# Attention and feed-forward layer: the product with v moves ahead of each half step's scores for the exponentials

## What is computed

```python
q, k, v = jnp.split(jnp.einsum('bld,ed->ble', x, w_qkv), 3, axis=-1)
q = _rope(q.reshape(B, L, H, Dh))
k = _rope(k.reshape(B, L, H, Dh))
scores = jnp.einsum('blhd,bmhd->bhlm', q, k) * scale
attn = jax.nn.softmax(scores, axis=-1)
out = jnp.einsum('bhlm,bmhd->blhd', attn, v).reshape(B, L, D)
return jnp.einsum('bld,ed->ble', out, w_out)
```

## Time and profile before

| | |
|---|---|
| median of 3 runs | 2955.85 us (2955.6 to 2956.34) |
| the profiled execution | 2953.22 us, its span 2951.4 us |
| busy share of the span | PE 97%, DVE 91%, ACT 83%, POOL 18% |
| chain that ended last | PE 87%, ACT 5%, DVE 5% |
| reductions of the maxima (L1289) | 2048, mean 1213 ns |
| exponentials (L893) | 4096, mean 595 ns |

### The profile page before, as it was taken

How to read it: one execution, slowest core, us unless ns; L and a number is a source line. 1 busy time by engine, 2 the same in 40 slices (tenths; PEclk the granted TensorE clock), 3 DMA queues, 4 the chain that set the end, 5 groups by cost and what they waited for, 6 DMA issues and landing times.

```text
span 2951.4 us, 67323 instructions
## 1 busy us (share of the span) xinstructions
PE 2860.2 (97%) x27416; PEld 1057.3 (36%) x27416; DVE 2683.4 (91%) x2910; ACT 2463.5 (83%) x4609; POOL 522.7 (18%) x1087
## 2 busy tenths in 40 slices
PE   5999997999999999999999999999999999999999
PEld 4566663233333333333333333333333333333336
DVE  6676667999999999999999999999999999999952
ACT  4545542899999999999999999999999999999972
POOL 4666662000000000000000000000000000000000
PEclk8999997899999999999999999999999999999999
DMA  3233231111111111111111111111111111111125
GB/s 108 82 105 113 91 106 51 26 32 31 31 31 30 31 31 32 31 32 31 31 31 31 31 31 31 31 31 31 31 31 31 31 31 31 31 31 31 31 63 179
DMA packets 124601, 137.14 MB, mean 46 GB/s; under 512 B 43264, under 2 KB 103296, under 8 KB 124288
## 3 DMA queue, kind: packets, MB, share of 16 engines
q1 hardware_dynamic: 124288, 132.79, 16.5%
HBM read 88.15 MB, written 34.08 MB: 41 GB/s over the span
## 4 chain that ended last, share of the span: by engine, by line
PE 87%; ACT 5%; DVE 5%; issue 2%; DMA 1%; SPq 0%; POOL 0%; DVEq 0%; ACTq 0%; POOLq 0%
PE psum L714 37%; PE psum L679 20%; PE psum L739 17%; PE psum L589 5%; PE psum L561 4%; ACT probs L893 3%; PE psum L662 2%; DVE row_max L1289 2%; ACT acc_sb L872 1%; PE psum L604 1%; ACT hT L796 1%; DVE stats L1061 1%; DVE xnT L1085 1%; DVE h L1213 0%; ACT silu L809 0%
## 5 line engine op out<-in xcount | busy, mean ns | idle before, releaser
L1289 DVE TENSOR_REDUCE row_max<-psum 128x1 f32<-128x1024 f32 x2048 | 2332.2, 1213 | 24.0 <-PE psum L679 23.0
L893 ACT ACTIVATE probs<-psum 128x512 f32<-128x512 f32 x4096 | 2179.2, 595 | 162.3 <-PE psum L739 59.6
L714 PE MATMUL psum<-probs,v_op 128*32 128x256 f32 x15872 | 1296.6, 398 | 0.0
L739 PE MATMUL psum<-q_op,k_op 51*128 51x512 f16 x4096 | 854.0, 381 | 19.1 <-ACT probs L893 15.6
L679 PE MATMUL psum<-k_op,q_op 48*128 48x512 f16 x4096 | 807.6, 391 | 21.3 <-DVE row_max L1289 19.8
L679 PEld LDWEIGHTS psum<-k_op,q_op 48*128 48x128 f16 x4096 | 196.6, 93 | 874.9 <-DVE row_max L1289 570.1
L714 PEld LDWEIGHTS psum<-probs,v_op 128*32 128x32 f32 x15872 | 312.4, 108 | 523.4 <-issue 484.8
L739 PEld LDWEIGHTS psum<-q_op,k_op 51*128 51x128 f16 x4096 | 365.1, 94 | 256.8 <-ACT probs L893 66.9
L1046 POOL TENSOR_TENSOR acc_sb<-acc_sb,inv_rows 128x512 f32<-128x512 f32 x64 | 81.7, 1276 | 1686.9 <-DMA inv_rows<-inv_dram 1686.9
L589 PE MATMUL psum<-xnT,wf 128*128 128x512 f16 x768 | 178.8, 379 | 0.0
L803 ACT ACTIVATE parts<-qk_rot 128x512 f16<-128x512 f32 x64 | 40.1, 627 | 147.6 <-POOL qk_rot L969 147.6
(11 more groups left out here) (103 smaller groups left out, 1025.1 us busy)
## 6 DMA issues: line engine op xcount, KB each, us to landing
qk_dram<-staged SPq DMA_DIRECT2D x64, 256.0 KB, 4.8
q_op<-qk_dram SPq DMA_DIRECT2D x128, 128.0 KB
k_op<-qk_dram SPq DMA_DIRECT2D x128, 128.0 KB
x_ln<-in_x SPq DMA_DIRECT2D x16, 512.0 KB, 4.3
x_res<-in_x SPq DMA_DIRECT2D x16, 512.0 KB, 5.1
y_dram<-y_blk SPq DMA_DIRECT2D x16, 512.0 KB, 3.3
k_op<-qk_dram SPq DMA_DIRECT2D x128, 64.0 KB
q_op<-qk_dram SPq DMA_DIRECT2D x128, 64.0 KB
```

The lines of the kernel that those rows point to most:

```text
L714: mm = pe.matmul(bank(7)[32 * j:32 * j + 32, n0:n1], v_op[:, h % 2, t, :], probs[:, g3 % PROBS, j * BANK + n0:j * BANK + n1], start=(t == ...
L739: pe.matmul(bank(b), k_op[r:e, h % SLOTS, t * P:(t + 1) * P], q_op[r:e, h % SLOTS, j * BANK:(j + 1) * BANK], start=True, stop=True).then_i ...
L893: nc.scalar.activation(probs[:, g2 % PROBS, j * BANK:(j + 1) * BANK], bank(b), ACT.Exp, scale=to_score).then_inc(s2_used, 1)
L1289: nc.vector.tensor_reduce(row_max[:, hl % 2, t, half:half + 1], psum[:, 2 * half * BANK:(2 * half + 2) * BANK], AX.X, ALU.max).then_inc(s1 ...
```

## The change

In each half step of the TensorE program the half product with v is issued ahead of the two scores for the exponentials, where it stood behind them. In the first half step it stands directly behind the first scores for the maxima, in the second directly behind the second ones, ahead of the stabiliser's transpose where there is one. Nothing else is touched: the same instructions, the same waits on each, the same buffers. The lists of the other engines are the same word for word.

```diff
+            weigh_v(0)
             for j in range(4):
                 if j == 2:
-                    weigh_v(0)
                     if c < N1:
                         max_half(c, 1)
+                    weigh_v(1)
                     h = head_of(c, STAB_AT)
                     if h is not None:
                         pe.wait_ge(stab_step, STAB_STEPS * (h + 1))
...
                     item += 1
-            weigh_v(1)
             if c > N1:
                 project(c - N1 - 1)
```

## The result

The change is slower: 2986.73 us, median of 4 runs (2986.06 to 2987.85), against 2955.72 (2955.35 to 2956.34) for the kernel before in the same runs. That is 31.0 us more, a ratio of 1.0105 (95% interval 1.0089 to 1.0121). Forecast were 2982.5 us, 26.7 more, in a range of 2957 to 2996, and slower with a chance of 0.8.

A forecast was written before the change was run, and what follows sets the result against it. TensorE's list was taken to set the pace, with VectorE close behind (24 us idle). Only the end of the head cost: 62 x 0.43 = 26.7 us on 2955.85 gave 2982.5 us, range 2957 to 2996.

The forecast's parts named there:

- The ordinary half step: Half steps without transpose or long product: the new order's distances 0.32, 0.57 and 0.22 make 1.11 us, as before; change 0.
- the first: Rival: the product with v starts sooner behind the maxima, making the kernel faster, put at 2940 us; chance 0.1.
- the third rival: Each exponentials' score behind v costs more than the maxima did; at 0.01 a half step +19, 3001 us; chance 0.1.
- the second rival: The second score's wait of 0.02 to 0.03 once a step is absorbed; 2958.5 us, no change; chance 0.1.
- The transpose: Transpose's half step: the second score waits for ScalarE until 1.39 either way, maxima at 1.61 against 1.63; change 0.
- The stabiliser's DMAs: Behind the transpose: the DMAs start 0.66 later, the first score needing them 0.67 later, so its wait stays; change 0.
- The end of the head: Across the long product: the next head's first product waits for ScalarE's late copy of bank 7; 4.15 against 3.72, +0.43 us.
- One for one, down to VectorE's floor: Time added to TensorE's list of a head counts fully; savings pay only until VectorE's 24 us of idle time.
- The sum: 62 heads of 0.43 us make +26.7 us, the rest 0; held within some 8 us with chance 0.7.

## Why the prediction was right, and where its sizes were off

*The ordinary half step: 0.* Right. The distances taken from the nearest rows (0.32, 0.57, 0.22) were measured as 0.31, 0.57 and 0.23, and the alternation of 1.11 and 1.14 stayed. That settles the first and the third rival: neither is the way into v cheaper behind the maxima, nor the exponentials' scores dearer behind v. The small wait once a step wasn't absorbed either, which was the second rival. The 24 quiet half steps are 0.03 longer, because one more of them is a half step of 1.14.

*The transpose: 0.* Right: 2.73 and 2.74. The rule of the Trainium skill that was weighed there (TensorEngine Tiling (Array Packing), Key Properties: a change of tiling mode drains TensorE) would have given 6 us, for three changes of mode instead of four. The trace shows nothing of it: the second score behind the transpose waits for ScalarE's exponential and starts 1.40 behind the maxima, where the forecast had 1.39. This doesn't speak against the rule, since a saving ahead of that score only lengthens its wait here; no run moves the number of changes at a place without such a wait.

*The stabiliser's DMAs: 0.* Off by a little, in the change's favour. The three half steps behind the transpose took 3.39 instead of 3.45, 0.06 a head or 4 us: the head's first score for the exponentials lost 0.05 to the DMAs before, and now doesn't (it starts 0.57 behind v, as in any half step). The forecast had the wait unchanged.

*The end of the head: +0.43.* The mechanism is right and stands row for row in the trace; it measured +0.55 on average. The expectation of the maxima behind it was 4.15, in the rows above it is 4.30, and three terms make the difference. The first exponential was put 0.42 behind its score; it is 0.49, because it carries the wait for `pv_done` as an instruction of its own (the run without that wait has 0.42, and its three half steps are 0.06 to 0.07 shorter). The earlier trace rows had this number: 1524.46 to 1524.94 is 0.48, and I took the 0.42 of an exponential in the middle of a step, thinking the 0.48 was ScalarE's backlog. From the end of the copy to the product that waits for it I put the 0.05 of a score behind an exponential; it is 0.10, and no run separates why. Two hundredths are the long product, 0.34 behind the maxima instead of 0.32.

*One for one, down to VectorE's floor.* Right for the change, too simple in general. With the long product back, TensorE's three half steps gained 0.42, and 0.33 of it was lost again, since VectorE had been starved in one piece and then set the pace. The floor isn't one number for the kernel; it starts anew wherever VectorE runs dry. The run with that order and without the wait confirms it.

The sum: 0.52 a head instead of 0.43, 31.0 us instead of 26.7. It came this close partly by luck: the end of the head was missed by 0.12 us, and the 0.06 gained at the DMAs hid half of that. Behind the last maxima, where the forecast allowed for one more 0.43 and left it out, the span grew by 2.4 us; no run separates why.

## What to carry to other kernels

When a loop's order is only rotated, look for the place where the pattern is irregular, since all of the price may be there. Here a once-a-head long product had doubled as the time in which ScalarE worked off two exponentials; with nothing handed to it beforehand it stood idle, and everything that came behind, a copy that another product needed, was late by as much. And before moving work to cover a wait, look whether the waits themselves are needed: a wait that another one already implies can be an instruction of its own on a nearly full engine, and taking this one away made the kernel before 14.5 us faster, while none of the orders tried beat that kernel by itself.

## What the runs showed that I had not expected

**A redundant wait costs ScalarE a gap.** In the kernel before, the two exponentials of a half step start 0.49 apart, and the second pair of a step starts 0.55 behind the last of the first pair. But the first of a step mostly starts 0.71 behind the last of the step before. In the same kernel without the wait both pairs start 0.62 behind. The timeline of ACT in the kernel before, three exponentials up to the step's end and the first two of the next:

```profile
1500.17 1.63 ACT L893 ACTIVATE probs<-psum 128x512 f32<-128x512 f32 x3
```
```profile
1501.92 1.08 ACT L893 ACTIVATE probs<-psum 128x512 f32<-128x512 f32 x2
```

The first row ends at 1501.80 and the next exponential starts at 1501.92, after 0.12 of idle time; within a row each starts up to 0.1 before the one ahead of it ends. Through the ring of three this had been the source of the 0.03 by which every second half step was longer: in the runs without the wait it is gone.

**TensorE's clock fell where it had stalled.** In the run with the long product alone moved, the granted clock falls to half (1.2 instead of 2.4 GHz) for a while, 13 times before the last maxima, once in three to five heads. The windows ahead of one, in it and behind it:

```profile
873.50:877.30 3.80, 2.89 (x22) 0.73 (x19) 2.56 (x4) 3.54 (x7) 0.00 (x0) 1.00 0.15 55
877.50:880.70 3.20, 3.20 (x24) 0.47 (x16) 2.15 (x2) 2.08 (x4) 0.00 (x0) 0.50 0.14 52
881.00:885.00 4.00, 4.00 (x48) 1.27 (x47) 4.00 (x4) 3.64 (x7) 0.00 (x0) 1.00 0.02 5
```

Ahead of it TensorE was busy for 2.89 of 3.80 us, with two waits for ScalarE in its timeline. Behind them come products like the last row, 0.61 long where 0.39 is usual:

```profile
874.41 0.39 PE L743 MATMUL psum<-q_op,k_op 51*128 51x512 f16 x1 [0.32 <-ACT probs L897]
...
875.88 0.39 PE L743 MATMUL psum<-q_op,k_op 51*128 51x512 f16 x1 [0.59 <-ACT probs L897]
...
878.29 0.61 PE L679 MATMUL psum<-k_op,q_op 48*128 48x512 f16 x2
```

The three half steps behind the stall take 1.5, 2.0 and 1.3 us in those heads instead of 1.11, 1.11 and 1.14: 1.5 us each time, some 20 us in all, about the 18 which that run took beyond my sum. The kernel before and the change have the clock at half for the first 51 and 48 us of the attention's maxima, and from there to the last maxima they have no such stretch. The same two waits, 0.32 and 0.59, stand in every head of this run, so the stall alone doesn't decide; why it fell behind these 13 and not behind the others is not shown. So an added stall on TensorE can cost more than its own length.
